# VectorE transposes the weighted sums and the heads of attention in 32x32 blocks, in place of TensorE, and a planner orders the work anew

## What is computed

```python
for l in range(LAYERS):
    keys = jnp.concatenate([past, x], axis=1)
    q, k, v = ...                                   # projections, 16 heads of 8
    scores = jnp.einsum('bqhd,bkhd->bhqk', q, k) / jnp.sqrt(HEAD_DIM)
    scores = jnp.where(valid[None, None], scores, neg)
    attn = jax.nn.softmax(scores, axis=-1)
    o = jnp.einsum('bhqk,bkhd->bqhd', attn, v).reshape(B, T, C)
    o = o @ Wo[l].T + bo[l]
    x = _ln(x + o, ln1_g[l], ln1_b[l])
    ff = jax.nn.gelu(x @ W1[l].T + b1[l], approximate=False) @ W2[l].T + b2[l]
    x = _ln(x + ff, ln2_g[l], ln2_b[l])
```

## Time and profile before

| | |
|---|---|
| median of 3 runs | 1104.46 us (1101.13 to 1105.72) |
| the profiled execution | 1104.54 us |
| its span, first to last instruction | 1102.7 us |
| mean granted clock of TensorE | 0.972 of full speed |
| instructions | 47422 |

### The profile page before, as it was taken

The page is one execution under the profiler, slowest core; times in us unless marked ns, Lnnn a source line. Parts: engine busy times, 40 slices in busy tenths (PEclk is TensorE's granted clock), DMA queues, the critical chain, the costliest instruction groups (busy, mean ns, idle before and its releaser), DMA issues.

```text
span 1102.7 us, 47422 instructions
## 1 busy us (share of the span) xinstructions
PE 994.2 (90%) x20080; PEld 705.4 (64%) x20080; DVE 809.7 (73%) x2451; ACT 763.1 (69%) x1418; POOL 407.5 (37%) x544
## 2 busy tenths in 40 slices
PE   1679999999999999999998999998987988899993
PEld 0356777777777777777775777666664544555772
DVE  6777887777778887777777775879798979872320
ACT  7457666767777667767773777767767868688741
POOL 8711433333344433333344213444646353401311
PEclk9769999999999999999998999999999989999997
DMA  5522211222225211332224123221112020401220
GB/s 160 116 62 61 61 42 42 78 70 61 62 62 105 56 43 41 64 89 62 61 62 103 27 38 61 60 46 29 35 28 60 3 61 4 117 26 37 68 77 10
DMA packets 72627, 64.80 MB, mean 59 GB/s; under 512 B 16226, under 2 KB 66914, under 8 KB 72418
## 3 DMA queue, kind: packets, MB, share of 16 engines
q1 hardware_dynamic: 72418, 61.78, 23.3%
HBM read 15.70 MB, written 1.05 MB: 15 GB/s over the span
## 4 chain that ended last, share of the span: by engine, by line
PE 72%; DVE 11%; ACT 5%; POOL 5%; issue 3%; SPq 1%; DMA 1%; POOLq 0%; DVEq 0%; ACTq 0%
PE b L775 11%; PE b L887 9%; PE b L878 8%; PE b L676 7%; PE b L756 5%; PE b L790 4%; PE b L959 4%; PE b L949 4%; PE b L709 4%; PE b L806 2%; PE b L846 2%; PE b L871 2%; DVE mx L1218 2%; ACT probs L1021 2%; PE b L862 2%
## 5 line engine op out<-in xcount | busy, mean ns | idle before, releaser
L1021 ACT ACTIVATE probs<-b 128x443 f32<-128x443 f32 (+2 forms) x736 | 354.0, 543 | 137.5 <-PE b L756 96.5
L1218 DVE TENSOR_REDUCE mx<-b 128x2 f32<-128x378 f32 (+1 forms) x768 | 353.0, 508 | 93.9 <-PE b L709 93.5
L676 PE MATMUL b<-band,identb 64*64 64x252 bf16 x2304 | 170.4, 286 | 18.4 <-DVE mx L1218 8.1
L775 PE MATMUL b<-probs,vals 128*32 128x189 f32 (+5 forms) x3968 | 182.8, 311 | 1.2 <-DVE mx L1218 0.3
L775 PEld LDWEIGHTS b<-probs,vals 128*32 128x32 f32 x3968 | 115.1, 110 | 47.2 <-issue 12.2
L1543 POOL TENSOR_SCALAR veps<-mv 128x4 f32<-128x4 f32 x48 | 11.0, 230 | 352.4 <-DVE mv L1324 352.4
L756 PE MATMUL b<-qpack,kpack 64*64 64x189 bf16 (+5 forms) x3968 | 137.0, 236 | 0.3 <-issue 0.3
L709 PE MATMUL b<-kpack,qpack 62*64 62x189 bf16 (+1 forms) x3072 | 122.0, 239 | 1.0 <-issue 1.0
L676 PEld LDWEIGHTS b<-band,identb 64*64 64x64 bf16 x2304 | 67.0, 105 | 83.6 <-issue 36.5
L887 PE MATMUL b<-w,hid 128*128 128x128 f32 x768 | 110.1, 287 | 0.0
L1215 DVE TENSOR_REDUCE mx<-b 128x1 f32<-128x512 f32 (+7 forms) x256 | 99.3, 444 | 14.1 <-PE b L724 13.7
(11 more groups left out here) (173 smaller groups left out, 1695.7 us busy)
## 6 DMA issues: line engine op xcount, KB each, us to landing
kpack<-kparts SPq DMA_DIRECT2D x168, 128.2 KB
qpack<-qparts SPq DMA_DIRECT2D x168, 128.0 KB, 3.4
qpack<-mrows SPq DMA_DIRECT2D x224, 4.0 KB
w<-in_w SPq DMA_DIRECT2D x12, 256.0 KB, 4.3
w<-in_wa SPq DMA_DIRECT2D x12, 256.0 KB, 3.3
w<-in_wb SPq DMA_DIRECT2D x12, 256.0 KB, 3.7
rowt<-in_rowt SPq DMA_DIRECT2D x6, 384.0 KB, 3.4
stream<-in_x SPq DMA_DIRECT2D x4, 256.0 KB, 4.0
```

What stands on the lines that cost most here:

```text
L676: pe.matmul(out, identb[rows, rows], rhs.unsqueeze(1).to_broadcast([64, 2, 2, EDGE]), start=True, stop=False, skip_group_check=True)
L775: mm = pe.matmul(bank("sum", u, group)[32 * j:32 * j + 32, q0:q0 + w - skip], vals[:, u % 2, at:at + 32], probs[:, n % SETS, j, col + skip ...
L1021: act.activation(probs[:, n % SETS, j, 0:width], bank("exp", u, v, b)[:, 0:width], ACT.Exp, scale=SCALE).then_inc(a_emptied, 1)
L1218: red = dve.tensor_reduce(out[:, 2 * tb:2 * tb + 2], read[:, 0:2 * width].rearrange("p (t k) -> p t k", k=width), AX.X, ALU.max)
```

## The change

The copies of the sums by ScalarE and the 12 transposes per unit by TensorE go. VectorE transposes each group of sums from its PSUM bank into SBUF (`turn_sums`, L1296 of the changed kernel), in blocks of 32x32: since each lane's sums lie in 32 rows of their own, tokens come to stand as rows inside each group of 32 rows and the lane's 32 values as columns. Reciprocals (L1301) and products (L1306) read SBUF, and one more block transpose (`turn_heads`, L1313) brings the heads back as rows, from which ScalarE writes ocat. The channels then stand in another order (`turned`), in which the output weights, the bias of v and the mask of active heads are laid out on the host. PSUM banks "heads" and "cat" are no longer used, and the bank of a sum is freed by VectorE.

The planner's costs are changed too (most by less than 10%, the building of the masks from 513 to 2000 ns), a change of tile form is charged when a job's start is worked out, a slack by tile form is added, BIAS and LATE get new numbers, many of them one for each place in a unit, and so every engine's order is a new one.

```diff
-TURN = {"q": 195, "k": 195, "out": 195, "hid": 195, "ffn": 195, "mixin": 195, "mixv": 195, "ehid": 195, "eout": 195,
-        "cat": 150, "turn": 150, "norm": 150, "rows": 150, "weigh": 140, "v": 250}
-TURN_LEAST, TABLE_LOAD = 95, 1400
...
+FIRST = {"q": 100, "k": 100, "out": 100, "hid": 100, "ffn": 100, "mixin": 100, "mixv": 100, "ehid": 100, "eout": 100,
+         "norm": 55, "rows": 55, "weigh": 45, "v": 150}
+TURN = {"pe": 95, "act": 1400}
+STAY = {"128x128": 256, "128x32": 13801, "128x64": 10817, "64x64": 0}
...
-BIAS = {"active": -97018, "add": -40065, "band": 33927, "blank": -9398, "bo": -13457, "bo_in": 127059,
...
+BIAS = {"add": (-270981, -288677), "back": 69446, "band": 320892, "blank": -116672, "bo": -656622, "bo_in": 113619,
...
-CAP = {"exp": 3, "heads": 8, "hid": 3, "max": 8}
+CAP = {"exp": 3, "hid": 8, "max": 8}
...
                     job = self.jobs[name]
-                    at = max(clock[e], soon[name])
+                    job.turns = job.mode is not None and mode[e] != job.mode
+                    at = max(clock[e] + (TURN[e] if job.turns else 0), soon[name])
...
+            def soon_enough(name):
+                job = self.jobs[name]
+                stay = STAY[job.mode] if e == "pe" and not job.turns else 0
+                return job.start <= at + max(SLACK[e], stay)
+
+            name = max(filter(soon_enough, open_[e]), key=worth)
...
-        add("act", ("sum", u, group), 487, [("weigh", u, group, banks_of(u) - 1), ("turn", u - 1, 1) if u else None],
-            frees=[("sum", u, group)], line="sum")
-    for half in range(2):
-        add("pe", ("turn", u, half), 435, [("sum", u, 1)], takes=[("heads", u, half)], mode=WIDE, line="turn")
-        add("dve", ("recip", u, half), 264, [("turn", u, half)], line="recip")
-        add("dve", ("heads", u, half), 341, [("recip", u, half), ("cat", u - 1) if u else None],
-            frees=[("heads", u, half)], line="heads")
-    add("pe", ("cat", u), 435, [("heads", u, 1)], takes=[("cat", u)], mode=WIDE, line="cat")
-    add("act", ("ocat", u), 600, [("cat", u), ("out", u - 1) if u else None, ("active",) if c else None],
-        frees=[("cat", u)], line="ocat")
-    add("pe", ("out", u), 889, [("ocat", u)], takes=[("out", u)], mode=WIDE, line="out")
+        add("dve", ("turn", u, group), 600, [("weigh", u, group, banks_of(u) - 1), ("ocat", u - 1) if u else None],
+            frees=[("sum", u, group)], line="turn")
+        add("dve", ("recip", u, group), 264, [("turn", u, group)], line="recip")
+        add("dve", ("heads", u, group), 341, [("recip", u, group)], line="heads")
+    add("dve", ("back", u), 600, [("heads", u, 1)], line="back")
+    add("act", ("ocat", u), 600, [("back", u), ("out", u - 1) if u else None, ("active",) if c else None], line="ocat")
+    add("pe", ("out", u), 920, [("ocat", u)], takes=[("out", u)], mode=WIDE, line="out")
...
-        otok, ocat = sb("otok", [P, TILES, P]), sb("ocat", [P, SEQ])
+        otok, ocat = sb("otok", [P, SEQ // 32, 2, 2 * HEAD]), sb("ocat", [P, SEQ])
...
-            def turn_sums(u, half):
-                out = bank("heads", u, half)
-                free(pe, ("heads", u, half))
-                if half == 0:
-                    pe.wait_ge(a_emptied, emptied("sum", u, 1))
-                for n in range(2):
-                    i = 2 * half + n
-                    for group in range(2):
-                        at = (2 * n + group) * P
-                        mm = pe.transpose(out[:, at:at + P], sums[:, group, i * P:(i + 1) * P], ident[:, :])
-                mm.then_inc(d_filled, 1)
-
-            def turn_heads(u):
-                out = bank("cat", u)
-                free(pe, ("cat", u))
-                pe.wait_ge(d_emptied, emptied("heads", u, 1))
-                for i in range(TILES):
-                    mm = pe.transpose(out[:, i * P:(i + 1) * P], otok[:, i, :], ident[:, :])
-                mm.then_inc(a_filled, 1)
-
             def project_out(u):
                 out = bank("out", u)
                 free(pe, ("out", u))
-                pe.wait_ge(a_emptied, emptied("cat", u))
+                pe.wait_ge(cat_ready, u + 1)
...
-            def copy_sums(u, group):
-                if u:
-                    act.wait_ge(d_filled, filled("heads", u - 1, 1))
-                act.wait_ge(summed, set_of(u, group, banks_of(u) - 1) + 1)
-                act.copy(sums[:, group, :], bank("sum", u, group)[:, :]).then_inc(a_emptied, 1)
...
-                act.wait_ge(a_filled, filled("cat", u))
+                act.wait_ge(heads_turned, u + 1)
                 if causal(u):
-                    act.activation(ocat[:, :], bank("cat", u)[:, :], ACT.Identity, bias=zero[:, 0:1],
-                                   scale=cols[:, par, COL_G1:COL_G1 + 1]).then_inc(a_emptied, 1)
+                    act.activation(ocat[:, :], sums[:, 0, :], ACT.Identity, bias=zero[:, 0:1],
+                                   scale=cols[:, par, COL_G1:COL_G1 + 1]).then_inc(cat_ready, 1)
                 else:
-                    act.activation(ocat[:, :], bank("cat", u)[:, :], ACT.Identity,
-                                   bias=cols[:, par, COL_BV:COL_BV + 1]).then_inc(a_emptied, 1)
+                    act.activation(ocat[:, :], sums[:, 0, :], ACT.Identity, bias=cols[:, par, COL_BV:COL_BV + 1]
+                                   ).then_inc(cat_ready, 1)
...
-            def invert(u, half):
-                read = bank("heads", u, half)[:, :].rearrange("p (n c) -> p n c", c=32)
-                dve.wait_ge(d_filled, filled("heads", u, half))
-                dve.reciprocal(recips[:, half, :, :], read[:, :, HEAD:HEAD + VW + 1:VW]).then_inc(recip_ready, 1)
-
-            def normalise_heads(u, half):
-                read = bank("heads", u, half)[:, :].rearrange("p (n c) -> p n c", c=32)
-                if u:
-                    dve.wait_ge(a_filled, filled("cat", u - 1))
-                dve.wait_ge(recip_ready, 2 * u + half + 1)
-                dve.tensor_tensor(otok[:, 2 * half:2 * half + 2, :].rearrange("p i (n e c) -> p (i n) e c", e=2, c=HEAD),
-                                  read[:, :, 0:BLOCK].rearrange("p n (e c) -> p n e c", c=VW)[:, :, :, 0:HEAD],
-                                  recips[:, half, :, :].unsqueeze(3).to_broadcast([P, 16, 2, HEAD]), ALU.mult
-                                  ).then_inc(d_emptied, 1)
+            def turn_sums(u, group):
+                if u and group == 0:
+                    dve.wait_ge(cat_ready, u)
+                dve.wait_ge(summed, set_of(u, group, banks_of(u) - 1) + 1)
+                dve.transpose(sums[:, group, :], bank("sum", u, group)[:, :]).then_inc(d_emptied, 1)
+
+            def invert(u, group):
+                read = sums[:, group, :].rearrange("p (i c) -> p i c", c=32)
+                dve.wait_ge(d_emptied, emptied("sum", u, group))
+                dve.reciprocal(recips[:, group, :, :], read[:, :, HEAD:HEAD + VW + 1:VW]).then_inc(recip_ready, 1)
+
+            def normalise_heads(u, group):
+                read = sums[:, group, :].rearrange("p (i c) -> p i c", c=32)
+                dve.wait_ge(recip_ready, 2 * u + group + 1)
+                dve.tensor_tensor(otok[:, :, group, :].rearrange("p i (e c) -> p i e c", c=HEAD),
+                                  read[:, :, 0:BLOCK].rearrange("p i (e c) -> p i e c", c=VW)[:, :, :, 0:HEAD],
+                                  recips[:, group, :, :].unsqueeze(3).to_broadcast([P, SEQ // 32, 2, HEAD]), ALU.mult
+                                  ).then_inc(heads_ready, 1)
+
+            def turn_heads(u):
+                dve.wait_ge(heads_ready, 2 * u + 2)
+                dve.transpose(sums[:, 0, :], otok[:, :, :, :].rearrange("p i g c -> p (i g c)")).then_inc(heads_turned, 1)
...
+    turned = np.arange(P).reshape(2, LANES, 2 * HEAD).transpose(1, 0, 2).reshape(P)
...
-        "wo": np.concatenate([T(each("Wo")), last("wo")]),
+        "wo": np.concatenate([T(each("Wo")), last("wo")])[:, turned],
```

141 lines of the change are left out of this document (85 added, 56 removed).

## The result

The changed kernel takes 1156.62 us (median of 4 runs, 1155.32 to 1156.96) against 1104.49 us for the kernel before on the same chip: a ratio of 1.0475 (95% interval 1.045 to 1.0499), 52 us slower. The forecast was 1067 us, with 0.06 for slower.

The account below looks back on a forecast made before the run. The prediction took TensorE (90% busy, 31.12 us a unit in the layers) to bound the kernel. It summed 1104.5 - 37.0 - 0.8 + 5 - 4.4 = 1067.3, so 1067 us, with a range of 1048 to 1089 us.

Parts of the forecast that it names:

- What goes from TensorE (-37.0): 12 transposes removed in each of 28 units give TensorE back 1.32 us a unit, 37.0 us in all.
- The waits for VectorE (+5, at most +29): TensorE's 49.7 us of waits for banks held by VectorE's row maxima grow by 5 us, at most 29.
- The cover of the earlier trace: 84.0 us of VectorE's maxima waiting for TensorE up to 740 us would absorb about 42 us of new VectorE work.
- ScalarE at nothing: Removing ScalarE's 56 copies of the sums (32.8 us) gains no time, as TensorE does not wait for ScalarE in the layers.
- The move from PSUM to SBUF at nothing: VectorE's 56 reciprocals and 56 products reading SBUF instead of PSUM were costed at nothing.
- The three uses of a PSUM bank a unit: Heads twice and cat once no longer compete with the maxima: a reason to put the added waits nearer the lower end.
- Changes of tile form (-0.8): TensorE's changes of tile form fall from 901 to 896 in the new order, 0.8 us less.
- The order at the end (-4.4): 8.7 us of TensorE work behind the last output projection moves earlier; half fills gaps, 4.4 us less.
- the transpose at 0.67 us: Each of VectorE's 84 new 128x512 block transposes takes 0.67 us, 56 us of busy time in all.
- 33 us less on ScalarE: ScalarE's busy time falls by about 33 us because the copies of the sums go.
- D: Rival: VectorE becomes the pace of the layers, a unit takes 32.3 us, total about 1132 us, slower; chance 0.06.
- E: Rival: the saved 37 us turn up as other TensorE idle time, sums' banks held longer; 1099 to 1110 us; chance 0.04.

Follow-up runs that it names:

- e14: e1 (order of the kernel before, block transposes on VectorE) with every PSUM bank use given its bank of the kernel before; 1133.7 us, ratio 1.0285.
- e15: e14 with each VectorE block transpose moving only 32 of its 512 columns (output not the reference's); 1116.3 us, ratio 1.0133.
- e19: e14 with 12 unused dummy transposes per unit put back on TensorE in units 4 to 20, where the removed ones stood; 1142.3 us, ratio 1.0374.
- e13: e7 with each VectorE block transpose moving only 32 of its 512 columns (output not the reference's); 1129.6 us, ratio 1.0258.
- e7: e4 with a one-column ScalarE activation added ahead of each table change, loading the next table early; 1130.9 us, ratio 1.024.
- e10: e1 with each VectorE block transpose moving only 32 of its 512 columns (output not the reference's); 1142.3 us, ratio 1.0375.
- e11: Kernel before with three unused VectorE transposes added in each of units 4 to 16, right behind the products of the heads; 1112.7 us, ratio 1.0097.
- e12: Kernel before with the same three transposes a unit as e11, but placed in a gap where VectorE waits for TensorE; 1103.4 us, ratio 1.0013.
- e6: Changed kernel, same orders and banks, with a one-column ScalarE activation that loads each next table early; 1134.5 us, ratio 1.0279.
- e4: Changed kernel with the rest of k (VectorE) and its lower parts (GpSimd) moved later in units 4 to 20, banks handed out anew; 1146.2 us, ratio 1.0406.
- e16: Kernel before, same instructions and order on every engine, only the PSUM banks handed out anew; 1129.4 us, ratio 1.0258.
- e1: Kernel before's order on every engine, but with the change's block transposes on VectorE, and banks handed out anew; 1146.6 us, ratio 1.0406.
- e2: Changed kernel's new order, but transposes left on TensorE and copies on ScalarE, banks handed out anew; 1194.8 us, ratio 1.085.
- e3: Changed kernel with the sums transposed in place in PSUM, so reciprocals and products read PSUM, banks handed out anew; 1164.4 us, ratio 1.0573.

## Why the prediction was wrong

- **What goes from TensorE (-37.0) with only +5 for new waits.** This is the step that failed, and it fails by itself: with the order and the banks of before the move costs 32 us (e14), and with VectorE's length nearly gone still 15 us (e15), where the sum had some 37 less. The prediction said that 37.0 us "can't fall as TensorE's work, only by new waits", and then priced new waits for VectorE alone. The price of one transpose was right, but its place was not read: the eight stood where the projections behind them had to wait for ScalarE's state, the four ahead of the output projection that waits for ocat. e19 pays 9 us for 22; scaled to 37 us, an estimate, some 15 were to be had, and e15's units show even less, 0.2 us of 1.32. The chain on TensorE all along showed that TensorE was never idle, not that it had nothing to cover.
- **The waits for VectorE (+5, at most +29).** This size failed too. The waits in question grew from 49.7 to 93.8 us in e14, by 44, with order and banks held, and to 133.6 in the changed kernel. VectorE's length was worth 17 us there (e14 against e15). The 1 us of e13 does not speak against it for the changed kernel, since e13 and e7 have other banks, and e10 shows how such banks hide it (4 us). The cover of the earlier trace rows was also taken as one sum, though the same work cost 10 us in one half of the unit and 1 in the other (e11, e12).
- **ScalarE at nothing.** The 56 copies were indeed not on the path, but the new order leaves the table loads behind waits: 22 us (e6). With the tables early the changed kernel stands at 1.0279 of before, and the move in the old order (e14) at 1.0285: the 20 us that the new order adds to the move are about what the late tables cost, though the two need not be the same microseconds.
- **The move from PSUM to SBUF at nothing.** The products doubled from 415 to 810 ns and the scaling rose by 85 ns, 22 and 17 us of busy time, next to GpSimd. What that costs in time is not shown: e4 gives 10 us, and only 4 once the tables are early (e7 against e6), but with other banks.
- **The three uses of a PSUM bank a unit** that no longer compete were counted as a small gain. That the hand-out of all other banks hangs on it was not seen. It can be worth 28 us (e16) and was worth 13 in e1, both brought in by `replay`; what the changed kernel's own banks cost or gain, no run shows.
- **Changes of tile form (-0.8)** were not measured apart. **The order at the end (-4.4)** had the right sign and size: 7 us behind the last heads.
- **Right:** the transpose at 0.67 us (0.70 measured), so the 56 us of VectorE time (59.0); 33 us less on ScalarE (32.3). The Trainium skill (TensorE: Matmul & The Clock Gate, Part 4: PE-mode transpose) gives about 275 ns for a 128x128 transpose in a kernel, a figure for bfloat16. An estimate from it would be 92 us less; the prediction rejected it with reason, since even 37 was too much.
- **Rivals.** D had the side and part of the mechanism: VectorE's length counts (17 us in e14), and 83% busy is where e14 stands in the layers (360.1 of 435.8 us). But its unit of 32.3 us is neither e14's 31.6 nor the changed kernel's 34.0, where three engines wait for each other in turn. E's "the saved 37 us turn up as other idle time" describes best what happened, with 0.04, too small a price and another reason. The chances failed with the sum: all rivals were priced on VectorE, and none on the waits that the transposes covered.

What stays open: the runs don't add up to 52 us, since each cost shows only when the others leave room (VectorE's length 1, 4 or 17 us; early tables 22, 15, 4 or -4 us). What the collision with GpSimd and the changed kernel's own banks are worth in its order is not shown, nor what the lower clock takes (mean 0.965 over the span against 0.972 before, 0.952 in e14).

## What to carry to other kernels

- Time saved on the busiest engine counts only where nothing it waits for stands right behind: for every removed instruction look at the next one and what that one would wait for. A bottleneck engine that is never idle may be covering latency with the very work that is taken away.
- Where buffers are handed out by a rule over the whole program, removing a few uses, moving one instruction or replaying an order by a slightly other rule can change many of them. Hold the old assignment and the old order fixed first, then judge the edit (e14), and compare the assignments use by use before a difference is put down to the edit: e2, e3 and e4 carry one that nobody had asked for.
- Read cover by place: a sum of waits over a stage says nothing about the half of the unit in which the new work lands.

## What the runs showed of the hardware

- VectorE's 32x32 block transpose of 128x512 float32 takes 0.71 us from PSUM and 0.70 from SBUF, and 0.21 us for 128x32 from PSUM (e10), so by these two sizes 1.04 ns a column above a start of 0.17 us.
- VectorE's product of two SBUF operands, normally 0.42 us, took up to 1.51 us when it started inside a GpSimd instruction with two SBUF operands, and ended soon after that (25 of 26 such products were long). Reading one operand from PSUM it stayed at 0.41 us (e3), and block transposes out of SBUF stayed at 0.70 us beside the same instructions.
- A table load (1.28 us) came with the first activation that needs it, behind that one's wait (383.60 us). One early activation of one column moved it ahead (e6: 1.1 us of idle time before 62 loads).
- In one ragged stage TensorE's granted clock was lower where TensorE had idled more: 0.75 in 20 us of which it was busy 11.6, 0.92 with 15.1. Idle time alone does not tell: from 538.5 to 760 us it was 0.98 before with 14.0 us idle, and 1.00 in the changed kernel with 24.3.
